# Inverse norms spread over the heads by bf16 selection matmuls in place of fp32 transposes, in a two-layer graph attention kernel

## The chip, the cores and the metric

One core of a Trainium2 chip runs the whole program. The metric is the device time of one execution in microseconds, the median of several; lower is better. Engines are named as in the profile: PE is TensorE (PEld its weight loads), DVE VectorE, ACT ScalarE, POOL GpSimd, SP SyncE, whose queue issues all DMAs.

## What is computed

128 graphs of 128 nodes with 512 features go through two pre-normed attention layers, each with a residual. The change touches only layer 0, where each node's feature vector is mapped, cut into 8 heads of 64, and normed per head to unit length; the cosine between two nodes gates the attention.

```python
m = embs @ map_w.T + map_b
sem = m.reshape(b, s, h, dk).transpose(0, 2, 1, 3)
norm = jnp.maximum(jnp.linalg.norm(sem, axis=-1, keepdims=True), COS_EPS)
n = sem / norm
cos = jnp.einsum('bhsd,bhtd->bhst', n, n)
cos_adj = (cos > THRESHOLD).astype(embs.dtype)
p_attn = jax.nn.softmax(scores, axis=-1) * keep      # scores from q and k of m
adj = cos_adj * p_attn
out = relu(((adj @ sem_h) @ gcn_W.T) / (adj.sum(-1, keepdims=True) + 1.0))
```

Layer 1 is a masked attention with 4 heads of 64 and an output projection.

## The kernel before, in words

Every matrix product with fp32 accuracy is made of three passes over f16 pairs: a tensor is kept as an upper half (rounded to f16 by ACT) and a lower half (the rest, subtracted by POOL or DVE), and PE multiplies upper by upper, upper by lower and lower by upper.

The program is unrolled over **slots**. Slot n treats graph n in its scores, cosines, softmax and gate, and works ahead or behind for the other stages. An even and the following odd slot together are a **pair**: the features of two graphs at once are made in it, with 256 moving columns. Each engine has its own hand-written list of steps per slot (`slot(s)`), and engines meet by semaphores only; an engine that waits holds everything behind it on its list. In PSUM, four banks (`unit_ps`) are given out in turn in the order of the table `UNITS`; a unit's bank is free when the step that reads it raises `unit_out`.

The order in an odd slot, as far as it matters here:

- PE (`slot`, behind L1357): scores (L1283, s_ps) and cosines (L1283, c_ps) of the slot's graph, q01, o1e (L1357), q23, weighted sums (L1323), o1o, norms (L1333), k01, lq, spread_inv_norm for graph 0 and for graph 1 (L1342), k23, lk, output (wo, L1273). The next slot, an even one, begins again with scores and cosines, then layer 1's scores, m, weighted sums, wo, va, lv, vb.
- DVE: scores_mask, q_features, o1_rows, gate (L889), o1_rows, norm_sums (L1002), attended, k_features 0 (L920), x1_stats, k_lower 0 (L943), lqk_lower of lq (L968), directions for graph 0 and 1 (L1016: m times the spread inverse norms), k_features 1, k_lower 1, lqk_lower of lk, result.
- ACT: x_rows, the exponentials (L708), o1_upper(5) and q's upper halves, e_upper, o1_upper(4) (L789, waits until the transposing DMA has read o_hl), k's upper half 0 (L797), lq's upper half (L822), the two directions_upper (L814), k's upper half 1, lk's, h1_rows, h1_upper.
- POOL: h1_lower, squares_last, keep_and_block, x_lower (L590), o1_lower(5) (L565), q_lower 0 (L597), inverse_norms, q_lower 1, e_lower (L576), directions_lower 0 and 1 (L638), norm_l1 (ve L647, nm L648, rstd L650, shift L652), o1_lower(4). In an even slot: h1_lower, v_lower, keep_and_block, result_bases (L559), p1_lower (L571), e_lower, p1_lower, norm_l1, norm_l0 (ve0, nm0, rstd0, shift0: L660, L661, L663, L665). DVE's square_rest (L1008) runs in the even slot too.
- SP: turn_h1, load_adj, load_residual, turn_x (L486, waits for x_lower), load_x, turn_o1 (L424), turn_e twice, store.

inverse_norms on POOL takes the 16 sums of squares per node (two graphs, 8 heads) to the power -1/2 (L625) and copies them out to [128 nodes, 2, 8, 64] (`inv_rows`, L631, one copy for each graph). PE then transposes inv_rows with fp32 transposes, four for each graph, so that a bank holds, for one graph, the factor of each of 512 features (rows) for each of 128 nodes (columns). The cosines wait only for the direction halves of their own graph (`dir_lo`, one count for each graph).

## Time and profile before

| | before |
|---|---|
| time, median of 3 (range) | 2671.84 us (2670.15 to 2672.61) |
| profiled execution: its time | 2665.52 us |
| profiled execution: its span | 2663.7 us, granted clock 0.981 on average |
| PE busy | 2566.1 us, 96% |
| DVE busy | 2060.3 us, 77% |
| ACT busy | 1710.0 us, 64% |
| POOL busy | 2168.1 us, 81% |
| DMA queue of all loads and turnings | 56.4% of 16 engines |
| chain that ended last | PE 89%, POOL 3%, DVE 3% |

Busy time is the sum over an engine's instructions. The granted clock is 1.00 in every stretch of 200 us from 200 to 2400 us; what is missing lies at the two ends, where the weights are prepared and the pipeline runs out. A timeline row gives start and duration in us, engine, line, operation, output and inputs, count, and in brackets the idle time before it with what ended it. Matmuls overlap in their records: 273 ns is the length of one with 256 columns, but they start 0.109 us apart.

### The profile page before, as it was taken

What the parts mean: (1) busy time and instruction counts of PE and PEld (TensorE: products, weight loads), DVE (VectorE), ACT (ScalarE), POOL (GpSimd) and SP (SyncE); (2) the same over time, 40 slices, a digit from 0 to 9 for tenths busy, and PEclk for the clock granted to TensorE, in tenths of its full rate; (3) what the DMA queues carried; (4) which work ended last, traced back from release to release, by engine and by line L of the source; (5) the groups of instructions that cost most, each with busy time, mean ns of one, the idle gap of its engine ahead of it and who ended that gap; (6) DMA issues with size and microseconds to landing.
All of it is one profiled execution on the core that took longest, in us unless ns stands there. A gap on an engine that the chain in (4) does not pass through costs nothing.

```text
span 2663.7 us, 78789 instructions
## 1 busy us (share of the span) xinstructions
PE 2566.1 (96%) x30681; PEld 2064.2 (77%) x30681; DVE 2060.3 (77%) x3456; ACT 1710.0 (64%) x4501; POOL 2168.1 (81%) x2449
## 2 busy tenths in 40 slices
PE   5789999999999999999999999999999999999995
PEld 3577888787788878878888887887888788788773
DVE  4267878878887888888788878888888878888873
ACT  1257667666766766766676676667667666766762
POOL 0368888888888888888888888888888888888873
PEclk7899999999999999999999999999999999999997
DMA  3145666556556656655665565566556556565643
GB/s 108 37 81 106 113 118 131 109 117 119 115 112 119 126 113 110 127 109 115 123 121 113 116 126 110 114 123 119 115 116 127 108 116 121 121 112 119 119 91 75
DMA packets 829123, 299.07 MB, mean 112 GB/s; under 512 B 772560, under 2 KB 778192, under 8 KB 828752
## 3 DMA queue, kind: packets, MB, share of 16 engines
q1 hardware_dynamic: 828752, 294.04, 56.4%
q8 instruction: 244, 4.00, 0.6%
q14 instruction: 127, 1.04, 0.1%
HBM read 75.80 MB, written 33.55 MB: 41 GB/s over the span
## 4 chain that ended last, share of the span: by engine, by line
PE 89%; POOL 3%; DVE 3%; ACT 2%; DMA 2%; issue 1%; SPq 1%; DVEq 0%; ACTq 0%; POOLq 0%
PE unit_ps L1265 47%; PE unit_ps L1273 24%; PE s_ps L1283 4%; PE s_ps L1323 3%; PE c_ps L1283 3%; PE unit_ps L1342 2%; PE unit_ps L1357 2%; PE unit_ps L1283 2%; PE unit_ps L1333 1%; POOL inv_norm L625 1%; DMA o_t<-o_hl 1%; ACT e_ec L708 1%; DVE qk_hl L943 1%; POOL inv_rows L631 1%; PE unit_ps L1234 1%
## 5 line engine op out<-in xcount | busy, mean ns | idle before, releaser
L708 ACT ACTIVATE e_ec<-e_ec,neg_mx 128x128 f32<-128x128 f32 x1024 | 397.9, 391 | 4.2
L1265 PE MATMUL unit_ps<-h_t,w_m_hi 128*128 128x256 f16 x2048 | 342.2, 274 | 9.5 <-DMA h_t<-h_hl 9.5
L1265 PE MATMUL unit_ps<-h_t,w_k_hi 128*128 128x256 f16 x2048 | 344.4, 273 | 0.0
L1265 PE MATMUL unit_ps<-h_t,w_q_hi 128*128 128x256 f16 x2048 | 342.8, 273 | 0.0
L1273 PE MATMUL unit_ps<-w_v_hi,h_t 128*128 128x512 f16 x1024 | 324.9, 379 | 0.0
L576 POOL TENSOR_TENSOR e_ec<-e_ec 128x1024 f16<-128x1024 f32 x128 | 287.6, 2247 | 15.7 <-ACT e_ec L735 15.7
L1265 PE MATMUL unit_ps<-h_t,w_m_lo 128*128 128x256 f16 x1024 | 280.4, 274 | 0.0
L1265 PE MATMUL unit_ps<-h_t,w_k_lo 128*128 128x256 f16 x1024 | 280.1, 274 | 0.0
L1265 PE MATMUL unit_ps<-h_t,w_q_lo 128*128 128x256 f16 x1024 | 279.1, 273 | 0.0
L943 DVE TENSOR_TENSOR qk_hl<-qk_sb,qk_hl 128x512 f16<-128x512 f32 x128 | 164.7, 1287 | 117.7 <-ACT qk_hl L797 117.6
L1265 PEld LDWEIGHTS unit_ps<-h_t,w_m_hi 128*128 128x128 f16 x2048 | 196.1, 98 | 39.0 <-issue 9.9
L920 DVE SCALAR_TENSOR_TENSOR qk_sb<-unit_ps,unscale,bias_q 128x512 f32<-128x512 f32 x128 | 96.1, 751 | 165.1 <-PE unit_ps L1265 163.8
L1265 PEld LDWEIGHTS unit_ps<-h_t,w_k_hi 128*128 128x128 f16 x2048 | 196.3, 98 | 21.8
L1265 PEld LDWEIGHTS unit_ps<-h_t,w_q_hi 128*128 128x128 f16 x2048 | 191.0, 98 | 27.2
L552 POOL TENSOR_TENSOR h_hl<-h_sb,h_hl 128x512 f16<-128x512 f32 x128 | 148.5, 1160 | 73.4 <-ACT h_hl L770 73.4
L625 POOL TENSOR_TENSOR inv_norm<-sq_sum,minus_half 128x16 f32<-128x16 f32 x64 | 186.5, 2914 | 26.4 <-DVE sq_sum L1002 26.4
L889 DVE SCALAR_TENSOR_TENSOR e_ec<-c_ps,e_ec 128x1024 f32<-128x1024 f32 x128 | 156.2, 1220 | 51.0 <-ACT e_ec L708 51.0
L708 ACT ACTIVATION_READ_ACCUMULATOR e_ec<-e_ec,neg_mx 128x1 f32 x1024 | 194.3, 190 | 0.0
L1273 PE MATMUL unit_ps<-w_v_lo,h_t 128*128 128x512 f16 x512 | 194.0, 379 | 0.0
L1273 PE MATMUL unit_ps<-w_o_hi,o_t 128*128 128x512 f16 x512 | 176.6, 386 | 14.5 <-DMA o_t<-o_hl 12.2
L1273 PEld LDWEIGHTS unit_ps<-w_v_hi,h_t 128*128 128x128 f16 x1024 | 100.2, 98 | 113.9
L797 ACT ACTIVATE qk_hl<-qk_sb 128x512 f16<-128x512 f32 x256 | 158.4, 625 | 46.4 <-DVE qk_sb L920 42.1
(175 smaller groups left out, 7722.7 us busy)
## 6 DMA issues: line engine op xcount, KB each, us to landing
xa<-in_x_dram SPq DMA_DIRECT2D x128, 256.0 KB, 3.4
xres<-in_x_dram SPq DMA_DIRECT2D x128, 256.0 KB, 2.8
out_dram<-ybuf SPq DMA_DIRECT2D x128, 256.0 KB, 2.5
h_t<-h_hl SPq DMA_TRANSPOSE x256, 3.2
ec_t<-e_ec SPq DMA_TRANSPOSE x256, 3.2
adj_in<-in_adj_dram SPq DMA_DIRECT2D x128, 16.0 KB, 2.0
p_t<-p_hl SPq DMA_TRANSPOSE x128, 3.3
o_t<-o_hl SPq DMA_TRANSPOSE x128, 3.8
```

Of the source, the lines that this page charges most:

```text
L552: nc.gpsimd.tensor_tensor(h1_hl[:, a, 1, :], h1_sb[:, a, :], h1_hl[:, a, 0, :], ALU.subtract).then_inc(h1_lo, 1)
L576: nc.gpsimd.tensor_tensor(e_hl[:, 1], e_sb[:, :, :], e_hl[:, 0], ALU.subtract).then_inc(e_lo, 1)
L625: nc.gpsimd.tensor_tensor(inv_norm[:, :], sq_sum[:, :], minus_half[:, :], ALU.pow).then_inc(inv_norm_done, 1)
L708: ins = nc.scalar.activation(e[:, h, :], e[:, h, :], ACT.Exp, bias=neg[:, h:h + 1], scale=SCALE, accum_out=sums[:, h:h + 1])
L797: nc.scalar.activation(dst[:, 0, c, :], src[:, c, :], ACT.Copy).then_inc(done, 1)
L889: nc.vector.scalar_tensor_tensor(out=e_sb[:, :, :], in0=c_ps[:, :, :].rearrange("p a (b n) -> p (a b) n", b=4), scalar=THRESHOLD * DIR_SCA ...
L920: nc.vector.scalar_tensor_tensor(out=dst[:, c0:c0 + 2, :], in0=unit_ps[:, u.bank, :].rearrange("p (c n) -> p c n", c=2), scalar=factor, in ...
L943: nc.vector.tensor_tensor(k_hl[:, 1, c, :], k_sb[:, c, :], k_hl[:, 0, c, :], ALU.subtract).then_inc(k_lo, 1)
L1265: ins = nc.tensor.matmul(out, w[a][:, i, c * P:(c + 1) * P], h[:, :, b, i, :], start=n == 0, stop=n == len(passes) - 1)
L1273: ins = nc.tensor.matmul(ps, h[:, a, i, :], w[b][:, i, :], start=n == 0, stop=n == len(passes) - 1)
L1283: ins = nc.tensor.matmul(outs[half][c], st[r, a, c, cols], mv[r, b, c, cols], start=n == 0, stop=n == 2)
L1323: ins = nc.tensor.matmul(av(p // 4)[:, p % 4, :], ec_t[:, a, p, :], v_sb[:, b, (s.n - 1) % 4, head_at(p), 0:DK + 1], start=n == 0, stop=n ...
```

## The change

The power stays. Behind it POOL splits the 16 inverse norms of a node into three bf16 parts (copy, subtract, copy, subtract: `inv_step`), in columns 0 to 23 of `inv_parts` for each of the two graphs. PE turns them with one matmul for each graph against a bf16 identity, into the unused part of the bank that `norms` has filled (`turn_inv_norm`). DVE copies these 256 columns to bf16 in SBUF (`inv_t`) and frees the bank. PE spreads them with four matmuls: `spread[:, c, :]` has ones in the rows of the three parts of heads 2c and 2c+1, so each sums the three parts and repeats them over the head's 64 features, for both graphs at once (256 columns). The banks bc0 and bc1 now hold blocks c = 0, 2 and 1, 3 of both graphs, where each held all blocks of one graph. Directions, their upper and their lower halves follow that split, so the cosines of the even slot wait for both counts of `dir_lo`. k23 moves ahead of the spread on PE, and k's second features and upper half move ahead of the directions on DVE and ACT. POOL's set-up gets two memsets, a copy and twelve selects.

```diff
-    (... ("norm", 1), ("k01", 1), ("lq", -3), ("bc0", 1), ("bc1", 1), ("k23", 1),
+    (... ("norm", 1), ("k01", 1), ("lq", -3), ("k23", 1), ("bc0", 1), ("bc1", 1),
...
+            nc.gpsimd.memset(inv_parts[:, :, :], 0.0).then_inc(ones_in, 1)
+            nc.gpsimd.memset(spread[:, :, :], 0.0).then_inc(ones_in, 1)
+            nc.gpsimd.tensor_copy(ident16[:, :], ident[:, :]).then_inc(ones_in, 1)
+            pool.wait_ge(ones_in, 5)
+            for part in range(3):
+                for c in range(C):
+                    ins = nc.gpsimd.affine_select(
+                        out=spread[:, c, :], in_=spread[:, c, :], compare_op=ALU.not_equal, fill=1.0,
+                        base=-(H * part + 2 * c), pattern=[[-1, 2], [0, DK]], channel_multiplier=1)
...
             def inverse_norms(s):
                 if s.has(1):
-                    u = s.unit("norm")
-                    pool.wait_ge(unit_out[u.bank], u.before + 1)
+                    pool.wait_ge(norm_summed, s.at(lambda t: (t + 1) // 2 + 1))
                     nc.gpsimd.tensor_tensor(inv_norm[:, :], sq_sum[:, :], minus_half[:, :], ALU.pow).then_inc(inv_norm_done, 1)
                     if s.has(-1):
-                        pool.wait_ge(unit_full, s.unit("bc1", back=2).full)
+                        pool.wait_ge(inv_turned, s.at(lambda t: (t + 1) // 2))
...
-                    for g in range(2):
-                        nc.gpsimd.tensor_copy(inv_rows[:, g], inv_norm[:, g * H:(g + 1) * H].unsqueeze(2).broadcast_to(
-                            [P, H, DK])).then_inc(inv_rows_done, 1)
+                    nc.gpsimd.tensor_copy(parts[0], inverse).then_inc(inv_step, 1)
+                    pool.wait_ge(inv_step, before + 1)
+                    nc.gpsimd.tensor_tensor(inv_rest[:, :, :], inverse, parts[0], ALU.subtract).then_inc(inv_step, 1)
+                    pool.wait_ge(inv_step, before + 2)
+                    nc.gpsimd.tensor_copy(parts[1], inv_rest[:, :, :]).then_inc(inv_step, 1)
+                    pool.wait_ge(inv_step, before + 3)
+                    nc.gpsimd.tensor_tensor(parts[2], inv_rest[:, :, :], parts[1], ALU.subtract).then_inc(inv_step, 1)
...
ACT
+                    qk_upper(s, "k", k_sb, k_hl, 1, k_hi)
                     directions_upper(s, 0)
                     directions_upper(s, 1)
-                    qk_upper(s, "k", k_sb, k_hl, 1, k_hi)
...
DVE
+            def inverse_turned(s):
+                if s.has(1):
+                    u = s.unit("norm")
+                    dve.wait_ge(inv_turned, s.at(lambda t: (t + 1) // 2 + 1))
+                    nc.vector.tensor_copy(inv_t[:, :], unit_ps[:, u.bank, P:3 * P]).then_inc(unit_out[u.bank], 1)
...
                     lqk_lower(s, "lq", lq_hl, LQ, 0)
+                    inverse_turned(s)
+                    k_features(s, 1)
                     directions(s, 0)
                     directions(s, 1)
-                    k_features(s, 1)
                     k_lower(s, 1)
...
PE
             def cosines(s):
                 if s.has(0):
-                    pe.wait_ge(dir_lo, s.at(lambda t: t + 1))
+                    pe.wait_ge(dir_lo, s.at(lambda t: 2 * (t // 2 + 1)))
...
-            def spread_inv_norm(s, g):
-                if s.has(1):
-                    pe.wait_ge(inv_rows_done, s.at(lambda t: t + 1 + g + 1))
-                    ps = start_unit(s, f"bc{g}")
+            def turn_inv_norm(s):
+                if s.has(1):
+                    pe.wait_ge(inv_step, s.at(lambda t: 4 * ((t + 1) // 2 + 1)))
+                    ps = unit_ps[:, s.unit("norm").bank]
+                    for g in range(2):
+                        ins = nc.tensor.matmul(ps[:, (g + 1) * P:(g + 2) * P], inv_parts[:, g, :], ident16[:, :],
+                                               start=True, stop=True)
+                    ins.then_inc(inv_turned, 1)
+
+            def spread_inv_norm(s):
+                if s.has(1):
+                    ps = [start_unit(s, f"bc{a}") for a in range(2)]
                     for c in range(C):
-                        ins = nc.tensor.transpose(ps[:, c * P:(c + 1) * P],
-                                                  inv_rows[:, g, 2 * c:2 * c + 2, :].rearrange("p h d -> p (h d)"), ident[:, :])
-                    ins.then_inc(unit_full, 1)
+                        ins = nc.tensor.matmul(ps[c % 2][:, c // 2 * 2 * P:(c // 2 + 1) * 2 * P], spread[:, c, :], inv_t[:, :],
+                                               start=True, stop=True)
+                        if c >= C - 2:
+                            ins.then_inc(unit_full, 1)
...
-                    spread_inv_norm(s, 0)
-                    spread_inv_norm(s, 1)
+                    turn_inv_norm(s)
                     qk_part(s, "k", w_k, 1)
+                    spread_inv_norm(s)
```

## Rows read from the trace of the kernel before

**Rows 1.** Windows: length, busy us (instructions) by engine, clock, DMA share, GB/s.

```profile
1332.79:1371.57 38.78, 38.78 (x479) 31.51 (x478) 31.35 (x54) 26.38 (x70) 33.97 (x39) 1.00 0.61 117
981.98:1022.04 40.06, 39.00 (x477) 31.43 (x476) 32.54 (x54) 26.39 (x70) 32.78 (x37) 1.00 0.63 114
280.96:2539.00 2258.04, 2252.02 (x27609) 1826.24 (x27608) 1833.64 (x3075) 1533.98 (x4060) 1963.79 (x2206) 1.00 0.60 117
```

**Rows 2.** Chain that ended last, one pair: start, us, what, count.

```profile
1320.19 5.26 PE unit_ps L1265 x48
```

**Rows 3.** Timeline of PE around the transposes of one pair.

```profile
1364.06 1.04 PE L1342 MATMUL unit_ps<-ident,inv_rows 128*128 128x128 f32 x8
1364.93 0.38 PE L1265 MATMUL unit_ps<-h_t,w_k_hi 128*128 128x256 f16 x2
```

**Rows 4.** Waits of the execution: who for whom, us, times, longest.

```profile
PE unit_ps L1265 <- DVE lq_hl L968: 9.8, 8, 1.7
...
SPq L486 <- POOL h_hl L590: 213.3, 64, 49.1
```

**Rows 5.** Timeline of POOL in the odd slot of the pair from 1332.79.

```profile
1359.99 2.91 POOL L625 TENSOR_TENSOR inv_norm<-sq_sum,minus_half 128x16 f32<-128x16 f32 x1 [0.43 <-DVE sq_sum L1002]
1363.04 1.18 POOL L631 COPY inv_rows<-inv_norm 128x512 f32<-128x512 f32 x2
1364.18 1.16 POOL L597 TENSOR_TENSOR qk_hl<-qk_sb,qk_hl 128x512 f16<-128x512 f32 x1
1365.29 2.58 POOL L576 TENSOR_TENSOR e_ec<-e_ec 128x1024 f16<-128x1024 f32 x1
1367.88 2.27 POOL L638 TENSOR_TENSOR dir_hl<-m_sb,dir_hl 128x512 f16<-128x512 f32 x2
```

**Rows 6.** Timeline of DVE in the same odd slot.

```profile
1359.40 0.42 DVE L993 TENSOR_TENSOR o_sb<-unit_ps,inv_lsum 128x256 f32<-128x256 f32 x1
...
1365.01 0.87 DVE L943 TENSOR_TENSOR qk_hl<-qk_sb,qk_hl 128x512 f16<-128x512 f32 x1 [1.74 <-ACT qk_hl L797]
1365.81 0.74 DVE L968 SCALAR_TENSOR_TENSOR lq_hl<-unit_ps,unscale,lq_hl 128x512 f16<-128x512 f32 x1
1366.47 1.27 DVE L1016 TENSOR_TENSOR m_sb<-m_sb,unit_ps 128x512 f32<-128x512 f32 x2
```

**Rows 7.** Timelines of POOL, DVE and PE in the pair from 981.98.

```profile
1014.49 2.13 POOL L576 TENSOR_TENSOR e_ec<-e_ec 128x1024 f16<-128x1024 f32 x1
...
1014.71 2.46 DVE L943 TENSOR_TENSOR qk_hl<-qk_sb,qk_hl 128x512 f16<-128x512 f32 x1 [2.05 <-ACT qk_hl L797]
...
1017.98 0.38 PE L1265 MATMUL unit_ps<-h_t,w_lk_hi 128*128 128x256 f16 x2 [1.06 <-DVE lq_hl L968]
```

**Rows 8.** Timelines of POOL and DVE in the pair from 1332.79, even slot.

```profile
1331.47 0.51 POOL L647 TENSOR_SCALAR ve<-mv 128x1 f32<-128x1 f32 x1
...
1333.04 0.19 POOL L652 TENSOR_TENSOR shift<-nm,rstd 128x1 f32<-128x1 f32 x1
...
1341.90 1.16 POOL L571 TENSOR_TENSOR p_hl<-p_sb,p_hl 128x512 f16<-128x512 f32 x1 [0.46 <-ACT p_hl L729]
...
1349.31 0.93 POOL L665 TENSOR_TENSOR shift<-nm,rstd 128x2 f32<-128x2 f32 x1
...
1354.00 2.28 POOL L590 TENSOR_TENSOR h_hl<-xa,h_hl 128x512 f16<-128x512 f32 x2
...
1348.97 1.22 DVE L1008 TENSOR_TENSOR sq_rest<-sq_t 128x1024 f32<-128x1024 f32 x1
```

**Rows 9.** Timelines of SP's queue and of ACT around the turned o_hl.

```profile
1358.99 1.20 SPq L424 DMA_TRANSPOSE o_t<-o_hl  x1
...
310.57 0.42 ACT L789 ACTIVATE o_hl<-o_sb 128x256 f16<-128x256 f32 x1 [2.02 <-DMA o_t<-o_hl]
...
2491.62 0.42 ACT L789 ACTIVATE o_hl<-o_sb 128x256 f16<-128x256 f32 x1 [4.11 <-DMA o_t<-o_hl]
```

**Rows 10.** ACT's upper halves over the execution: busy us, mean ns, idle.

```profile
L814 ACT ACTIVATE dir_hl<-m_sb 128x512 f16<-128x512 f32 x128 | 78.7, 632 | 120.3 <-DVE m_sb L1016 120.3
```

More of the change, by code:

```diff
@@ L64 @@
     (("s1a", -4), ("s1b", -4), ("m01", 2), ("m23", 2), ("wo", -5), ("va", 2), ("lv", -4), ("vb", 3)),
-    (("q01", 1), ("o1e", -5), ("q23", 1), ("o1o", -4), ("norm", 1), ("k01", 1), ("lq", -3), ("bc0", 1), ("bc1", 1), ("k23", 1),
+    (("q01", 1), ("o1e", -5), ("q23", 1), ("o1o", -4), ("norm", 1), ("k01", 1), ("lq", -3), ("k23", 1), ("bc0", 1), ("bc1", 1),
      ("lk", -3), ("wo", -5)),
@@ L236, in build @@
         sq_parts = (sq_halves[:, :, :, 1], rest_halves[:, :, :, 1], sq_halves[:, :, :, 0])
-        inv_rows = sb("inv_rows", [P, 2, H, DK])
+        inv_rest = sb("inv_rest", [P, 2, H])
+        inv_parts = sb("inv_parts", [P, 2, P], BF16)
+        inv_t = sb("inv_t", [P, 2 * P], BF16)
+        spread = sb("spread", [P, C, P], BF16)
+        ident16 = sb("ident16", [P, P], BF16)
         lq_hl = sb("lq_hl", [P, 2, C1, 2 * P], F16)
@@ L325, in build @@
         inv_norm_done = sem("inv_norm_done")
-        inv_rows_done = sem("inv_rows_done")
+        norm_summed = sem("norm_summed")
+        inv_step = sem("inv_step")
+        inv_turned = sem("inv_turned")
         masked = sem("masked")
@@ L388, in build @@
         SMALL_LOADS = 7
-        ONES = 4
+        ONES = 10
         L_AT = 2 * C
@@ L541, in _ @@
             nc.gpsimd.memset(lv_sb[:, 1, :, :, DH:DH + 1], 0.0).then_inc(ones_in, 1)
+            nc.gpsimd.memset(inv_parts[:, :, :], 0.0).then_inc(ones_in, 1)
[7 more added lines that the diff above has]
+                        base=-(H * part + 2 * c), pattern=[[-1, 2], [0, DK]], channel_multiplier=1)
+                ins.then_inc(ones_in, 1)
+                pool.wait_ge(ones_in, 6 + part)
             pool.wait_ge(largest_done, 1)
@@ L622, in inverse_norms @@
                 if s.has(1):
-                    u = s.unit("norm")
-                    pool.wait_ge(unit_out[u.bank], u.before + 1)
+                    pool.wait_ge(norm_summed, s.at(lambda t: (t + 1) // 2 + 1))
                     nc.gpsimd.tensor_tensor(inv_norm[:, :], sq_sum[:, :], minus_half[:, :], ALU.pow).then_inc(inv_norm_done, 1)
                     if s.has(-1):
-                        pool.wait_ge(unit_full, s.unit("bc1", back=2).full)
+                        pool.wait_ge(inv_turned, s.at(lambda t: (t + 1) // 2))
+                    before = s.at(lambda t: 4 * ((t + 1) // 2))
+                    inverse = inv_norm[:, :].rearrange("p (g h) -> p g h", g=2)
+                    parts = [inv_parts[:, :, H * i:H * (i + 1)] for i in range(3)]
                     pool.wait_ge(inv_norm_done, s.at(lambda t: (t + 1) // 2 + 1))
-                    settle(pool, settled_pool, s.i)
-                    for g in range(2):
-                        nc.gpsimd.tensor_copy(inv_rows[:, g], inv_norm[:, g * H:(g + 1) * H].unsqueeze(2).broadcast_to(
-                            [P, H, DK])).then_inc(inv_rows_done, 1)
+                    nc.gpsimd.tensor_copy(parts[0], inverse).then_inc(inv_step, 1)
[5 more added lines that the diff above has]
+                    nc.gpsimd.tensor_tensor(parts[2], inv_rest[:, :, :], parts[1], ALU.subtract).then_inc(inv_step, 1)
             def directions_lower(s, g):
                 if s.has(1):
-                    cols = slice(g * P, (g + 1) * P)
                     pool.wait_ge(dir_hi, s.at(lambda t: t + 1 + g + 1))
-                    nc.gpsimd.tensor_tensor(dir_hl[:, 1, :, cols], m_sb[:, :, cols], dir_hl[:, 0, :, cols],
+                    nc.gpsimd.tensor_tensor(dir_hl[:, 1, g::2, :], m_sb[:, g::2, :], dir_hl[:, 0, g::2, :],
                                             ALU.subtract).then_inc(dir_lo, 1)
@@ L812, in directions_upper @@
                         wait(act, c_full, s.at(lambda t: t + 1))
-                    cols = slice(g * P, (g + 1) * P)
-                    nc.scalar.activation(dir_hl[:, 0, :, cols], m_sb[:, :, cols], ACT.Copy).then_inc(dir_hi, 1)
+                    nc.scalar.activation(dir_hl[:, 0, g::2, :], m_sb[:, g::2, :], ACT.Copy).then_inc(dir_hi, 1)
             def lqk_upper(s, name, dst, k):
@@ L1013, in directions @@
                     u = s.unit(f"bc{g}")
-                    cols = slice(g * P, (g + 1) * P)
                     dve.wait_ge(unit_full, u.full)
-                    nc.vector.tensor_tensor(m_sb[:, :, cols], m_sb[:, :, cols],
-                                            unit_ps[:, u.bank, :].rearrange("p (c n) -> p c n", c=C),
+                    nc.vector.tensor_tensor(m_sb[:, g::2, :], m_sb[:, g::2, :],
+                                            unit_ps[:, u.bank, :].rearrange("p (c n) -> p c n", c=2),
                                             ALU.mult).then_inc(unit_out[u.bank], 1)
```

2 lines of the change are left out of this document (1 added, 1 removed).

## The prediction

> **What bounds the kernel now.** I read the windows first. In a stretch that is one pair of graphs (an even and an odd slot, from one start of the scores in an even slot to the next) the PE column equals the length of the stretch, 38.78 of 38.78 us, at a granted clock of 1.00 [rows 1]. Pairs 2 to 59 take 2258.04 us together, 38.93 on average [rows 1]: 0.15 us above the pair that has no gap. So TensorE sets the end, every column streamed costs time, and nothing else does until PE has to wait. Then I looked for what stands closest behind PE. The list of waits has PE at w_lk behind the low half of lq (DVE, L968) 8 times, and it has SyncE's queue at the turning of h (L486) behind GpSimd's x low halves in all 64 pairs [rows 4]. The timelines of one pair (start 1332.79; from here +x is us after a pair's start) give the distances. POOL ends the power at +30.11, copies inv_rows until +31.43, takes the low half of q, then that of e (2.58 us), then the two of the directions until +37.36 [rows 5]. PE starts the eight transposes at +31.27 and k23 0.87 us later [rows 3]. POOL is the engine to watch, since it has 33.97 us of work in 38.78 [rows 1].
>
> **PE's own work.** Removed: 8 fp32 transposes, 0.87 us, 0.109 each [rows 3]. Added: 4 spread matmuls with 256 moving bf16 columns. 48 f16 matmuls of 256 columns took 5.26 us, 0.11 each [rows 2], so 0.44 us. The 2 turning matmuls have 128 columns: half of that is 0.055; the bounds are nothing and the 0.109 of a transpose [rows 3]. I take 0.055, since cost here goes by columns: 0.11 together (0 to 0.22). Sum 0.55 for 0.87: 0.32 us less a pair (0.21 to 0.43), 18.6 us over the 58 pairs, some 20 in all. Everything below is what can eat this.
>
> **The wait for the three parts.** PE now waits for four small POOL operations in a chain in place of one copy. The nearest rows are shift, 0.19 us for one element, with a gap of some 0.08 before it [rows 8], and, far above, 0.59 for a copy of 512 [rows 5]. From +30.25: four at 0.19 to 0.22 and three gaps come to 1.05, so +31.30, and PE can turn at +31.36 in place of +31.27: 0.09 us lost (0 to 0.3). Behind the turn nothing else on PE is early: a plain pair becomes 38.78 - 0.32 + 0.09 = 38.55 us.
>
> **The wait for inv_t.** The spread stands one k23 (24 matmuls, 2.62 us) behind the turn: +31.36 + 0.11 + 2.62 = +34.09. Its operand is copied by DVE behind k's first low half and lq's low half, which ended +33.76 in this pair [rows 6]. The copy of 256 PSUM elements isn't in the trace; the 256-element o_sb took 0.42, and 512 elements of lq_hl took 0.74 [rows 6]: 0.42, with 0.74 as the upper bound and 0.3, where the line through both has its lower reach at some 160 elements, as the lower. It ends at about +34.0: in a plain pair just in time. Before, the thing that waited for lq's low half was w_lk at +34.76, so 1.0 us of slack is gone and 0.3 us of copy is put in.
>
> **What a late pair costs.** k's low half (L943) took 0.87 us here and 2.46 us in the late pair [rows 6, 7]: there it was issued after POOL's e_ec had started, ran on until after e_ec had ended, and PE stood 1.06 us at w_lk [rows 7]. That pair took 40.06 us, 1.28 more than a plain one [rows 1]. The Trainium skill says why ("SBUF — State Buffer", section "Who interferes with whom"): a DVE instruction with two SBUF inputs and a GpSimd instruction that reads SBUF exclude one another, and the one that came first keeps the port to its end. The trace agrees, in both directions (shift0 took 0.93 us under DVE's sq_rest, its like 0.19 [rows 8]). After the change, in such a pair: POOL's q half ends +32.42, e_ec (2.13 [rows 7]) +34.5, k's half 0.55 later, lq's half +35.7, the copy +36.08, PE starts the spread at +36.14 in place of +34.09. A late pair loses 2.05 us and takes 40.6.
>
> **Where the moved directions put POOL.** k's second features and its upper half now come before the directions. k23's result comes at +34.30; DVE then needs 0.74 and, for the directions, 1.27 [rows 6] to +36.24, ACT's last upper half (0.63 each [rows 10]) ends +36.9, and DVE takes the port for k's second low half at about +36.2 to +36.8, ahead of POOL. POOL's two direction halves, 2.27 together [rows 5], then end at some +38.97, 0.42 after the next pair's start at +38.55, where they ended 1.42 before it. That is 1.84 us later on POOL's queue, seen from the next pair. The norm of layer 1 behind them gives 0.32 back (ve took 0.51 under the lock, else 0.19 [rows 8]), leaving 1.5. Everything on POOL's queue behind it moves. The only idle place in the even slot is 0.46 us ahead of p_hl [rows 8]; about 1.0 stays. So norm_l0 reaches its nm0 just after DVE has begun sq_rest (1348.97 [rows 8]); now only shift0 is caught by it, then three of its four steps stand behind it, and it ends some 1.15 later. With dir_lo ahead of k's half the figure at p_hl is 0.6, and the rstd0 step is still caught: 0.95 later. The queue has no idle until x's low halves (1354.00 [rows 8]). SyncE waits for these in each pair [rows 4], and turn_o1 (1358.99 [rows 9]) stands behind them, so it is issued about 1.1 us later. ACT's second o_hl, and behind it k's upper half, wait for that transfer.
>
> **How many pairs become late.** Read from ACT's timeline, o_hl L789 of o1_upper(4) starts between +29.6 (310.57) and +32.0 in 57 pairs, median +30.6; one late one is at 2491.62 [rows 9]. k's low half follows 0.97 us later and is caught by e_ec if o_hl is later than about +31.4: 7 of 57 now. Moved by 0.95 to 1.15 us it would be 60 to 75%. DMA waiting may soak up some of the move, so I take 60%: 0.4 x 38.55 + 0.6 x 40.6 = 39.78, which is 0.85 above 38.93. Times 58 = 49 us, less 1 for the pairs at the ends: +48. The new set-up on POOL (two memsets, a copy, twelve selects) runs while DVE and POOL wait for weights; I cost it at nothing (0 to 3 us if that cover is gone).
>
> The profiled execution has a span of 2663.7 and a time of 2665.52 us; the sum is a difference and I put it on the median, 2671.84: **2720 us**. With 40% late pairs it is +25, with 80% +72: 2697 to 2744.
>
> **Rivals.** (a) POOL's lateness is absorbed: if the small ends differ by half a microsecond, norm_l0 gets its steps in before sq_rest, x's low halves start on time, and late pairs stay at 7 of 57. Then 0.88 x 38.55 + 0.12 x 40.6 = 38.80, -0.13 x 58 = -8: 2664; with no late pair at all 38.55, -22: 2650. For it: each link is tenths of a microsecond, and DMA landings scatter by 2.4 us. Against it: the 1.8 us shift is three to four times the idle place. 27%. (b) The mid case, 20 to 40% late, 2673 to 2697: 10%. (c) Slower still: every pair is caught, 40.6, +97 us, 2769, if the transfer lands 2 us later; it decides where o_hl never starts before +31.4: 5%. (d) The change doesn't save on PE because a small bf16 turn costs as much as a transpose: 0.21 for 0.32 a pair, 6 us; it moves all cases and isn't one of its own. The forecast has 58%.
>
> Measurement of this kernel can tell 0.2%, 5.3 us, from no change. Faster 0.26 (most of a), same 0.08, slower 0.66. The range for 8 in 10 is 2655 to 2745; the likeliest case alone spans 2697 to 2744.
>
> **What would show it.** Right: the eight L1342 rows are gone and the turn and spread stand at 0.11 and 0.44; PE has gaps of some 2 us before the spread, put down to DVE's inv_t copy, in over a third of pairs; DVE's k low half takes over 2 us in these; POOL's norm_l0 steps are longer and x's low halves start about 1 us later after a pair's start. Wrong: pairs of 38.5 us throughout, POOL's direction halves done before the next pair's start, or turn_o1 issued at the same +26.2 as now.

## The result, and the profile after

Times are medians; each ratio is to runs of the kernel before on the same chip, with its 95% interval.

| | before | after |
|---|---|---|
| time, median (range) | 2670.99 us (2664.76 to 2674.53) | 2731.95 us (2722.3 to 2735.63) |
| ratio | | 1.0223 [1.0199, 1.0246] |
| profiled execution: span, granted clock | 2663.7 us, 0.981 | 2730.8 us, 0.980 |
| mean of pairs 2 to 59 of the profiled execution | 38.93 us | 39.89 us |
| PE busy | 2566.1 us, 96% | 2559.6 us, 94% |

The change makes the kernel 2.2% slower, 61 us. The forecast was 2720, with 2655 to 2745 around it.

First the page of after: the span, the busy time of each engine, and the shares of the chain that ended last.

```profile
span 2730.8 us, 78689 instructions
...
PE 2559.6 (94%) x30553; PEld 2033.8 (74%) x30553; DVE 2058.0 (75%) x3520; ACT 1708.8 (63%) x4501; POOL 2144.6 (79%) x2592
...
PE 44%; POOL 27%; DVE 7%; DMA 7%; issue 7%; SPq 5%; ACT 3%; ACTq 0%; POOLq 0%; DVEq 0%
```

PE is busy for 6.5 us less and the profiled execution takes 67 us more. Before, 89% of the last chain was PE; now it is 44%, and 27% is POOL. So work was taken from the engine that set the end, and the end passed to a loop through POOL. The windows of two successive pairs and of pairs 2 to 59 together (columns as in [rows 1]; pairs are numbered as in the prediction, so that pair 0 is the third of the 64 in the trace):

```profile
370.04:408.60 38.56, 38.56 (x477) 31.05 (x478) 30.75 (x55) 26.40 (x70) 33.38 (x41) 1.00 0.57 119
408.60:449.14 40.54, 38.70 (x477) 30.93 (x476) 31.26 (x55) 26.43 (x70) 33.55 (x41) 1.00 0.59 112
...
290.87:2604.27 2313.40, 2243.21 (x27493) 1797.53 (x27492) 1831.16 (x3133) 1533.20 (x4060) 1937.64 (x2321) 1.00 0.58 114
```

A plain pair has shrunk from 38.78 to 38.56 and PE still has no gap in it. A late one takes 40.54 with PE busy for 38.70. In the 58 pairs PE is idle for 70.2 of 2313.40 us (before, 6.0 of 2258.04 [rows 1]). I count a pair as late when DVE's first low half of k ends past +34.5: 38 of 58, against 5 of 58 before. The list of waits names what they wait for (who, for whom, us, times, longest):

```profile
PE unit_ps L1376 <- DVE inv_t L1029: 73.3, 40, 1.8
...
PE unit_ps L1368 <- POOL inv_parts L654: 9.3, 6, 3.7
```

L1376 is the spread, L1368 the turn. The late pair from 1443.5 shows how the wait comes about. DVE, PE and POOL, start and duration in us:

```profile
1476.11 2.46 DVE L963 TENSOR_TENSOR qk_hl<-qk_sb,qk_hl 128x512 f16<-128x512 f32 x1 [2.11 <-ACT qk_hl L818]
1478.49 0.74 DVE L988 SCALAR_TENSOR_TENSOR lq_hl<-unit_ps,unscale,lq_hl 128x512 f16<-128x512 f32 x1
1479.15 0.41 DVE L1029 CAST inv_t<-unit_ps 128x256 bf16<-128x256 f32 x1
```

```profile
1474.88 0.28 PE L1368 MATMUL unit_ps<-ident,inv_parts 128*128 128x128 bf16 x2
1475.01 0.38 PE L1291 MATMUL unit_ps<-h_t,w_k_hi 128*128 128x256 f16 x2
...
1479.62 0.61 PE L1376 MATMUL unit_ps<-inv_t,spread 128*128 128x256 bf16 x4 [1.83 <-DVE inv_t L1029]
1480.07 0.38 PE L1291 MATMUL unit_ps<-h_t,w_lk_hi 128*128 128x256 f16 x2
```

```profile
1470.72 2.92 POOL L641 TENSOR_TENSOR inv_norm<-sq_sum,minus_half 128x16 f32<-128x16 f32 x1 [0.45 <-DVE sq_sum L1022]
1473.77 0.20 POOL L648 CAST inv_parts<-inv_norm 128x16 bf16<-128x16 f32 x1
1474.05 0.22 POOL L650 TENSOR_TENSOR inv_rest<-inv_norm,inv_parts 128x16 f32<-128x16 f32 x1
...
1474.61 0.22 POOL L654 TENSOR_TENSOR inv_parts<-inv_rest,inv_parts 128x16 bf16<-128x16 f32 x1
...
1475.90 2.13 POOL L593 TENSOR_TENSOR e_ec<-e_ec 128x1024 f16<-128x1024 f32 x1
```

The three parts are done at +31.32 and the turn starts at +31.37, 0.10 later than the transposes did before. But DVE's k half was issued at 1476.11, 0.2 us after e_ec had started, and ran on until 0.54 us after its end: 2.46 us, the same length as in the one late pair read from before [rows 7]. The copy of inv_t stands two places behind it, and PE waits 1.83 us for it.

Why it is issued late is seen in the even slot. POOL in the pair from 1402.94, norm_l0:

```profile
1419.03 0.19 POOL L681 TENSOR_SCALAR ve<-mv 128x2 f32<-128x2 f32 x1
1419.30 1.13 POOL L682 TENSOR_SCALAR nm<-mv 128x2 f32<-128x2 f32 x1
1420.52 0.72 POOL L684 TENSOR_TENSOR rstd<-ve,minus_half 128x2 f32<-128x2 f32 x1
1421.32 0.19 POOL L686 TENSOR_TENSOR shift<-nm,rstd 128x2 f32<-128x2 f32 x1
```

nm, for two elements, takes 1.13 us here; it was issued at +16.4, just behind DVE's sq_rest, which starts at +16.19 in both kernels. Before, only shift0 was caught there [rows 8]. So x's low halves start at +22.33 after a plain pair instead of +21.21, the turning of o_hl is issued at a median of +27.29 instead of +26.22 [rows 9], and ACT's o_hl starts at a median of +31.70 instead of +30.57. The k half follows 0.97 us behind it and, in 38 pairs, is issued after e_ec has started.

Where the 67.0 us of span are: 58 pairs at 0.954 more make 55.3; pairs 0 and 1, both late, 3.2; the stretch before pair 0, which starts at 209.9 instead of 203.2, 6.7; the tail 1.8.

### The profile page after: what moved, and what is told of

Its sections match the earlier page's. It is cut to its first block, busy times and chain, and to the rows that moved or that the text cites. A ratio compares the mean times of both kernels' runs of the same rounds, so it can differ in the third digit from the quotient of the medians.

```text
span 2730.8 us, 78689 instructions
## 1 busy us (share of the span) xinstructions
PE 2559.6 (94%) x30553; PEld 2033.8 (74%) x30553; DVE 2058.0 (75%) x3520; ACT 1708.8 (63%) x4501; POOL 2144.6 (79%) x2592
## 3 DMA queue, kind: packets, MB, share of 16 engines
q14 instruction: 129, 1.06, 0.1%
## 4 chain that ended last, share of the span: by engine, by line
PE 44%; POOL 27%; DVE 7%; DMA 7%; issue 7%; SPq 5%; ACT 3%; ACTq 0%; POOLq 0%; DVEq 0%
PE unit_ps L1291 22%; PE unit_ps L1299 12%; DMA o_t<-o_hl 7%; DVE qk_hl L963 3%; POOL ybuf L576 3%; POOL p_hl L588 3%; POOL h_hl L607 3%; POOL h_hl L569 3%; POOL v_sb L599 2%; SPq L492 2%; POOL dir_hl L659 2%; POOL sq_t L636 2%; SPq L501 2%; PE s_ps L1309 2%; PE c_ps L1309 2%
## 5 line engine op out<-in xcount | busy, mean ns | idle before, releaser
L659 POOL TENSOR_TENSOR dir_hl<-m_sb,dir_hl 128x512 f16<-128x512 f32 x128 | 165.8, 1314 | 184.7 <-ACT dir_hl L834 184.7
L593 POOL TENSOR_TENSOR e_ec<-e_ec 128x1024 f16<-128x1024 f32 x128 | 281.7, 2201 | 10.0 <-ACT e_ec L756 10.0
L963 DVE TENSOR_TENSOR qk_hl<-qk_sb,qk_hl 128x512 f16<-128x512 f32 x128 | 149.3, 1167 | 129.1 <-ACT qk_hl L818 129.1
L810 ACT ACTIVATE o_hl<-o_sb 128x256 f16<-128x256 f32 x128 | 52.4, 409 | 257.8 <-DMA o_t<-o_hl 255.7
L783 ACT ACTIVATE h_sb<-x,shift,rstd 128x512 f32<-128x512 f32 x128 | 104.1, 813 | 170.1 <-POOL shift L673 170.1
L641 POOL TENSOR_TENSOR inv_norm<-sq_sum,minus_half 128x16 f32<-128x16 f32 x64 | 186.5, 2914 | 27.4 <-DVE sq_sum L1022 27.3
```

The lines of the kernel that those rows point to most:

```text
L593: nc.gpsimd.tensor_tensor(e_hl[:, 1], e_sb[:, :, :], e_hl[:, 0], ALU.subtract).then_inc(e_lo, 1)
L641: nc.gpsimd.tensor_tensor(inv_norm[:, :], sq_sum[:, :], minus_half[:, :], ALU.pow).then_inc(inv_norm_done, 1)
L659: nc.gpsimd.tensor_tensor(dir_hl[:, 1, g::2, :], m_sb[:, g::2, :], dir_hl[:, 0, g::2, :], ALU.subtract).then_inc(dir_lo, 1)
L783: nc.scalar.activation(h1_sb[:, a, :], x1[:, (s.n - 1) % 8, :], ACT.Relu, bias=shift1[:, 0:1], scale=rstd1[:, 0:1]).then_inc(h1_done, 1)
L963: nc.vector.tensor_tensor(k_hl[:, 1, c, :], k_sb[:, c, :], k_hl[:, 0, c, :], ALU.subtract).then_inc(k_lo, 1)
```

## The experiments

Pairs are counted as above, 58 in each kernel; the last three columns are of one profiled execution each. "Plain" and "late" are the usual (median) lengths of the two kinds. The kernel before, run beside them on the same chips, had medians from 2665.53 to 2670.99 us, so kernels are compared by their ratios where microseconds would mix chips.

| run | kernel | median us | ratio | mean pair | late | plain / late us |
|---|---|---|---|---|---|---|
| e1_copy_first | after, inv_t copied first | 2711.34 | 1.0157 [1.0137, 1.0177] | 39.51 | 42 | 38.55 / 39.87 |
| e2_norm_first | after, norm_l1 and o1_lower(4) ahead of the directions | 2696.12 | 1.0101 [1.0084, 1.0117] | 39.37 | 9 | 39.14 / 41.14 |
| e3_both | e1 and e2 | 2691.19 | 1.0076 [1.0059, 1.0092] | 39.27 | 10 | 39.14 / 40.46 |
| e8_all | e3, o1_upper(4) later, set-up later | 2683.03 | 1.0046 [1.0029, 1.0063] | 39.15 | 0 | 39.14 / none |
| e9_norm_alone | after, norm_l1 alone ahead | 2666.35 | 0.9997 [0.9984, 1.0009] | 38.86 | 7 | 38.56 / 40.57 |
| e10_all_norm_alone | e8, o1_lower(4) back behind | 2648.17 | 0.994 [0.9927, 0.9952] | 38.56 | 0 | 38.56 / none |
| e12_after_o1_late | after, o1_upper(4) later | 2672.67 | 1.0022 [1.0012, 1.0031] | 38.95 | 0 | 38.94 / none |
| e11_before_o1_late | before, o1_upper(4) later | 2675.33 | 1.003 [1.0017, 1.0043] | 39.08 | 0 | 39.06 / none |
| e4_order | before, only the changed order | 2683.2 | 1.0062 [1.0041, 1.0083] | 39.27 | 23 | 38.78 / 40.00 |
| e5_fill1 | before, one copy more on POOL | 2672.88 | 1.0025 [1.0006, 1.0044] | 39.28 | 22 | 38.78 / 40.06 |
| e6_fill2 | before, two copies more | 2724.98 | 1.0216 [1.0195, 1.0238] | 39.91 | 44 | 38.8 / 40.27 |
| e7_setup | before, only the new set-up | 2665.42 | 0.9998 [0.9985, 1.001] | 38.92 | 5 | 38.78 / 40.06 |

The theory: POOL's two direction halves end past the pair's end and put the norms behind them late (the lateness); the lateness reaches x's low halves and, by SyncE and the turned o_hl, ACT's o_hl and k's low half; e_ec catches that; and the inv_t copy makes what is lost there 2.0 us instead of 1.28. The first three runs cut that chain at two places.

### The copy of inv_t first

DVE, odd slot:

```diff
+                    inverse_turned(s)
                     k_lower(s, 0)
                     lqk_lower(s, "lq", lq_hl, LQ, 0)
-                    inverse_turned(s)
```

> The changed kernel with DVE's copy of inv_t moved ahead of k's first low half and lq's low half. Theory (late pairs come from GpSimd's late queue, their price from the copy's place behind DVE's port wait): still 60 to 70% late pairs, but each stalls PE only at w_lk, by about 1.25 us in place of 2.0, so a late pair takes 39.8 us in place of 40.57 and the kernel some 30 us less than the changed one, near 2703. Rival (the chain power, three parts, turn, copy is itself what delays PE): the copy then starts as soon as the turn is done, the gaps vanish wholly, pairs of 38.56 throughout, near 2660.

The waits of e1:

```profile
PE unit_ps L1291 <- DVE lq_hl L988: 54.3, 46, 1.7
```

The wait for inv_t is gone from the late pairs and the wait of before, for lq's low half [rows 4], is back in its place, 46 times. No fewer pairs are late (42, where after has 38), but a late one takes 39.87, 1.3 over a plain one, which is what it cost before [rows 1]. So the place of the copy makes a late pair dearer by 0.7, and is not why pairs are late.

### The norm of layer 1 ahead of the directions

POOL, odd slot:

```diff
+                    norm_l1(s)
+                    o1_lower(s, 4)
                     directions_lower(s, 0)
                     directions_lower(s, 1)
-                    norm_l1(s)
-                    o1_lower(s, 4)
```

> The changed kernel with norm_l1 and o1_lower(4) ahead of the two directions_lower on GpSimd in the odd slot, where GpSimd idles some 2.9 us. Theory (GpSimd's queue is late by 1.5 us because the directions end late; this passes through norm_l0 and x's low halves to the transfer of o_hl): x's low halves are back at +21.2 after a pair's start, turn_o1 at +26.2, late pairs fall from 39 of 58 to 6 to 9 of 58 at an unchanged 40.57, mean pair 38.8, the kernel near 2672. Rival (late pairs come from the new inv_norm chain and where DVE's k half falls beside it): the share of late pairs stays, near 2730.

> Both edits of the last two kernels. Theory: 6 to 9 late pairs of 58 at 39.8 us, the others 38.56, mean 38.7, near 2667 (of it some 8 us more than before at the two ends). Rival: as for the first kernel, no late pair at all.

The share of late pairs fell from 38 to 9 and 10 of 58, as expected. The time came out 24 us above what I expected in both. The waits of e2, and POOL about 401.72:

```profile
PE c_ps L1309 <- POOL dir_hl L659: 18.7, 42, 0.9
PE unit_ps L1376 <- DVE inv_t L1029: 18.3, 10, 1.8
```

```profile
401.72 0.63 POOL L673 TENSOR_TENSOR shift<-nm,rstd 128x1 f32<-128x1 f32 x1
402.31 0.67 POOL L582 TENSOR_TENSOR o_hl<-o_sb,o_hl 128x256 f16<-128x256 f32 x1
402.94 2.27 POOL L659 TENSOR_TENSOR dir_hl<-m_sb,dir_hl 128x512 f16<-128x512 f32 x2
```

A wait had taken the place of the one removed: the next slot's cosines need both directions, and o1_lower(4), 0.67 us, now stands ahead of them. Plain pairs are 39.14, 0.58 over 38.56. I had moved two functions where the argument needed one, and my expectations had not costed the second.

### The norm alone

```diff
+                    norm_l1(s)
                     directions_lower(s, 0)
                     directions_lower(s, 1)
-                    norm_l1(s)
                     o1_lower(s, 4)
```

> The changed kernel with norm_l1 alone ahead of the two directions_lower on GpSimd; o1_lower(4) stays behind them. In e2 most plain pairs took 39.14 us in place of 38.56: PE stood 0.58 us at the cosines for the directions' low halves, which o1_lower(4) had pushed 0.66 us back. Theory: without it that wait is gone, plain pairs are 38.56 to 38.6, and GpSimd's lateness is still gone, since layer 1's h no longer waits for it: x's low halves at +21.2, 5 to 10 late pairs of 58 at 40.57, mean 38.8 to 38.9, near 2675. Rival (o1_lower(4), late by the directions, keeps GpSimd late): x's low halves 0.8 to 1.1 us late and 23 to 38 late pairs, near 2715 to 2730.

The window of pairs 2 to 59 of e9 and its wait at the spread:

```profile
286.53:2540.69 2254.16, 2238.20 (x27493) 1799.92 (x27493) 1807.57 (x3133) 1521.97 (x4061) 1949.37 (x2321) 1.00 0.61 117
```

```profile
PE unit_ps L1376 <- DVE inv_t L1029: 12.8, 7, 1.8
```

One function moved on POOL's queue brings the ratio from 1.0223 to 0.9997, some 60 us: x's low halves start at +21.21 again in every pair, 7 pairs are late, and plain pairs are 38.56. The directions still end 0.58 us past the pair's end (+39.14), so it is what is queued behind them, not their own end, that makes pairs late. This shows the chain's first half. It is also rival (a) of the prediction, brought about: 7 late of 58 gave a mean of 38.86 (it said 38.80). But the kernel as a whole is level with before, where (a) had 8 us less: of the 4 us that the 58 pairs give back, the ends take all, since pair 0 starts at 209.6.

### ACT's o_hl behind k's upper half

The second half of the chain, from x's low halves to the k half, is cut by this, in after (e12) and in before (e11). ACT, odd slot:

```diff
-                    o1_upper(s, 4)
                     qk_upper(s, "k", k_sb, k_hl, 0, k_hi)
                     lqk_upper(s, "lq", lq_hl, LQ)
+                    o1_upper(s, 4)
```

> The changed kernel with the same edit alone. Theory: no late pair; k's first low half is issued at about +30.4, between the four small steps of inv_norm, and holds the port 0.55 us, so the turn is 0.5 us late: pairs of about 39.05, near 2680, although GpSimd's queue is as late as in the changed kernel. Rival (GpSimd's lateness costs by itself, by another way than the transfer of o_hl): pairs still near 39.9 on average, near 2730.

> The kernel before with ACT's o1_upper(4) behind the upper halves of k and lq, so that nothing of theirs waits for the transfer of o_hl. It asks whether the kernel before could have had the gain of e10 without the bf16 spread. Theory: no late pair is left, but DVE issues k's first low half at about +30.4 in each pair, takes the port between GpSimd's two copies of inv_norm, the second ends 0.45 us late and the second four transposes wait some 0.28: pairs of 39.06 throughout, 7 us more over 58 pairs, near 2673. Rival: PE never waits, 38.78 throughout, 9 us less, near 2657.

In e12 x's low halves are as late as in after, at +22.32, and no pair is late. So POOL's lateness makes pairs late only by way of the o_hl that ACT waits to write. All pairs take 38.94 instead of 38.56, though (I expected 39.05), and in e11 39.06, as expected. DVE and POOL in one pair of e12, POOL's row at the same place in a pair of e11, and the wait of e12:

```profile
474.57 0.66 DVE L963 TENSOR_TENSOR qk_hl<-qk_sb,qk_hl 128x512 f16<-128x512 f32 x1
...
474.70 0.60 POOL L650 TENSOR_TENSOR inv_rest<-inv_norm,inv_parts 128x16 f32<-128x16 f32 x1
```

```profile
546.72 1.63 POOL L631 COPY inv_rows<-inv_norm 128x512 f32<-128x512 f32 x2
```

```profile
PE unit_ps L1368 <- POOL inv_parts L654: 27.6, 64, 3.7
```

The k half, freed, comes so early that it now holds up POOL's splitting (0.60 for an operation that takes 0.22 in after), or, in before, the copies (1.63 for two that take 0.59 each [rows 5]); PE waits 27.6 us for the parts, over 64 pairs, instead of 9.3. So the kernel before could not have had a gain from this edit alone: e11 is 0.3% slower than before.

### All of it

Both ACT and DVE edits, norm_l1 with and without o1_lower(4) ahead of the directions, and the set-up behind the first all-reduce:

```diff
+            pool.wait_ge(largest_done, 1)
+            nc.gpsimd.partition_all_reduce(top[:, 0:1], largest[:, 0:1], P, RED.absmax).then_inc(top_done, 1)
             nc.gpsimd.memset(inv_parts[:, :, :], 0.0).then_inc(ones_in, 1)
...
-            pool.wait_ge(largest_done, 1)
-            nc.gpsimd.partition_all_reduce(top[:, 0:1], largest[:, 0:1], P, RED.absmax).then_inc(top_done, 1)
```

> Both edits, ACT's o1_upper(4) behind k's and lq's upper halves so that these no longer wait for the transfer of o_hl, and GpSimd's set-up of the selection matrices behind its first all-reduce, where it idles. Theory: k's first low half is always issued while q's low half holds the port, no late pair is left, all pairs 38.56, 21 us less than before over 58 pairs, the first pair 2 us earlier than in the changed kernel; near 2653. Rival (DMA landing isn't the cause of late pairs): the late pairs that e3 has remain, 5 to 10 us above that.

> The kernel of e8 (copy of inv_t first on DVE, ACT's o1_upper(4) behind the upper halves of k and lq, set-up behind the first all-reduce) with o1_lower(4) back behind the directions. Theory: no late pair, no wait at the cosines, every pair 38.56: 0.59 x 58 = 34 us less than e8, near 2650, 0.7% faster than before. Rival (the cosines' wait for both graphs stays, by GpSimd's port wait): 39.0 us pairs, near 2675.

The waits of e8:

```profile
PE c_ps L1309 <- POOL dir_hl L659: 28.6, 64, 1.3
```

Then the page of e10, its window of pairs 3 to 60, its wait for the directions, and POOL and DVE in one odd slot:

```profile
span 2645.9 us, 78689 instructions
...
PE 2552.0 (96%) x30553; PEld 2038.1 (77%) x30553; DVE 2015.3 (76%) x3520; ACT 1700.1 (64%) x4501; POOL 2159.2 (82%) x2592
```

```profile
322.32:2558.96 2236.64, 2236.42 (x27495) 1800.44 (x27494) 1788.09 (x3129) 1522.59 (x4057) 1946.89 (x2315) 1.00 0.61 118
```

```profile
PE c_ps L1309 <- POOL dir_hl L659: 2.9, 3, 1.1
```

```profile
1047.16 0.22 POOL L650 TENSOR_TENSOR inv_rest<-inv_norm,inv_parts 128x16 f32<-128x16 f32 x1
...
1047.72 0.22 POOL L654 TENSOR_TENSOR inv_parts<-inv_rest,inv_parts 128x16 bf16<-128x16 f32 x1
```

```profile
1048.32 0.42 DVE L1029 CAST inv_t<-unit_ps 128x256 bf16<-128x256 f32 x1 [1.21 <-PE unit_ps L1368]
1048.66 0.94 DVE L963 TENSOR_TENSOR qk_hl<-qk_sb,qk_hl 128x512 f16<-128x512 f32 x1
```

e8 has no late pair, but each waits for the cosines (39.14), and it ends 30 us above what I expected; that expectation was on record before e2 had shown the wait. e10 has neither wait: PE is busy for 2236.42 of 2236.64 us, each pair takes 38.56, and at 0.994 [0.9927, 0.9952] (2648 us, expected 2650) it beats both kernels. Its DVE waits for the turn, which comes after all three parts, before it takes up the k half: the splitting is back at 0.22, and the collision of e12 can't happen. A pair without gaps is thus 0.22 us shorter by the change, 13 us over 58; most of the rest of the 0.6% is that the 5 late pairs of before are gone too. The 2.2% came from late pairs, and these from what stood behind the directions on POOL's queue.

### Order, lateness and set-up, each alone

e4 is before, with only k23 and its followers moved ahead of the spread and the directions; the fp32 transposes stay:

```diff
-    (... ("lq", -3), ("bc0", 1), ("bc1", 1), ("k23", 1),
+    (... ("lq", -3), ("k23", 1), ("bc0", 1), ("bc1", 1),
...
+                    qk_upper(s, "k", k_sb, k_hl, 1, k_hi)
                     directions_upper(s, 0)
                     directions_upper(s, 1)
-                    qk_upper(s, "k", k_sb, k_hl, 1, k_hi)
...
+                    k_features(s, 1)
                     directions(s, 0)
                     directions(s, 1)
-                    k_features(s, 1)
...
+                    qk_part(s, "k", w_k, 1)
                     spread_inv_norm(s, 0)
                     spread_inv_norm(s, 1)
-                    qk_part(s, "k", w_k, 1)
```

> The kernel before with the order alone changed: k23 ahead of the transposes on PE, k's second features and upper half ahead of the directions on DVE and ACT; fp32 transposes and the copies of inv_norm stay. Theory (order makes GpSimd late): a plain pair stays 38.78, x's low halves 0.8 to 1.1 us later, about 60% late pairs, each 1.28 us as before since only w_lk waits: +35 us, near 2706. Rival (the three parts and the copy of inv_t are the cause): late pairs stay 5 of 58, near 2671.

The waits of e4:

```profile
PE unit_ps L1265 <- DVE lq_hl L968: 30.4, 27, 1.7
```

The order alone makes 23 pairs late and costs 0.6%: the sign is as expected and the size half of it. Plain pairs here are 0.22 longer, so the directions end exactly at the pair's end and the lateness is less: x's low halves start at +22.02 after a plain pair, 0.80 late where after has 1.12. Behind a late pair it is the other way round, +22.33 in e4 and +22.01 in after, and the means are the same (22.15 and 22.12). The edge lies later, too. A pair is late if the k half, 0.97 us behind o_hl's start, is issued after e_ec has started, and e_ec starts when POOL's low half of q ends: +32.55 in before and in e4, +32.43 in after. For o_hl that is +31.58 and +31.46. Counted by these edges, o_hl is too late in 5 pairs of before, 22 of e4 and 38 of after, where 5, 23 and 38 are late. Held against e4's edge, +31.58, after would still have 35, so the edge accounts for 3 of the 15 pairs between them. The rest lies in when o_hl starts, a median of +31.40 in e4 and +31.70 in after, for x's low halves that are equally late on average. The difference stands behind plain pairs (13 of 34 late in e4, 18 of 19 in after), where after's low halves are 0.31 later; behind late pairs it is 9 of 23 and 20 of 38, although e4's are the later ones. One profiled execution of each does not settle this, and why e4 has so few late pairs stays open.

e5 and e6 put lateness into before without touching the order: one or two copies of 512 elements (nothing reads the result) behind the directions.

```diff
+            def pool_filler(s):
+                if s.has(1):
+                    for g in range(1):
+                        nc.gpsimd.tensor_copy(filler[:, g], inv_norm[:, 0:H].unsqueeze(2).broadcast_to([P, H, DK]))
...
                     directions_lower(s, 1)
+                    pool_filler(s)
                     norm_l1(s)
```

> The kernel before with one more copy of 512 elements (0.6 us, into a tile that nothing reads) on GpSimd behind directions_lower. Theory (0.5 us of lateness is absorbed in the even slot): x's low halves stay at +21.2, late pairs 5 to 10 of 58, within 6 us of before. Rival (no threshold, each delay on GpSimd costs in proportion): about half of the effect of two copies.

> The same with two copies (1.2 us). Theory: lateness of about 1.3 us at the next pair, 0.75 behind the idle place, norm_l0's second step caught by DVE's sq_rest, x's low halves 0.8 to 1.0 later, some 60% late pairs at 40.06: +35 us (20 to 50), near 2706. Rival (GpSimd lateness isn't passed on to the transfer): within 6 us of before.

POOL in e5, norm_l0 in a pair behind a plain one (571.62 to 572.73) and in one behind a late one (1164.38, 1166.41), and DVE's sq_rest in the first of them:

```profile
571.62 0.23 POOL L667 TENSOR_SCALAR nm<-mv 128x2 f32<-128x2 f32 x1
571.93 0.72 POOL L669 TENSOR_TENSOR rstd<-ve,minus_half 128x2 f32<-128x2 f32 x1
572.73 0.81 POOL L671 TENSOR_TENSOR shift<-nm,rstd 128x2 f32<-128x2 f32 x1
...
1164.38 1.15 POOL L667 TENSOR_SCALAR nm<-mv 128x2 f32<-128x2 f32 x1
...
1166.41 0.19 POOL L671 TENSOR_TENSOR shift<-nm,rstd 128x2 f32<-128x2 f32 x1
...
572.28 1.22 DVE L1015 TENSOR_TENSOR sq_rest<-sq_t 128x1024 f32<-128x1024 f32 x1
```

The copy took 1.07 us instead of the 0.6 that I had put in. Even so, the lateness behind a plain pair stops just short of sq_rest: nm gets in, only shift is caught, and x's low halves start at +21.21 as before. Behind a late pair it is 0.8 more, nm is caught, and they start at +22.33. So lateness feeds itself: of 22 pairs behind a late one 16 are late, of 35 behind a plain one 6. The kernel's time scatters accordingly, from 2663.04 to 2686.89, and its profiled execution lies at the upper end, so its 39.28 us a pair is no mean of its runs. That feedback I had not expected; in the profiled execution 22 pairs are late where I had 5 to 10. With two copies, 1.7 us in all, x's low halves start at +22.33 behind most plain pairs (nm caught), and at about +22.9 behind all late ones, where norm_l1's shift is caught already and all four steps of norm_l0 come after sq_rest. 44 pairs are late: 58 us where I expected 35. Before's order with 1.7 us of POOL work added is as slow as after.

e7 is before with the two memsets, the copy and the twelve selects of the set-up alone:

```diff
+            nc.gpsimd.memset(inv_parts[:, :, :], 0.0).then_inc(ones_in, 1)
+            nc.gpsimd.memset(spread[:, :, :], 0.0).then_inc(ones_in, 1)
+            nc.gpsimd.tensor_copy(ident16[:, :], ident[:, :]).then_inc(ones_in, 1)
...
+                    ins = nc.gpsimd.affine_select(
```

> The kernel before with only the set-up of the change on GpSimd (two memsets, a cast, twelve selects; their tiles are not used). The profile of the changed kernel has its second pair of features start later, the first all-reduce 3.0 us later than before. Theory: the set-up itself costs 2 to 3 us of the time. Rival (the delay of the first all-reduce is a late load, the set-up is hidden): 0.

It costs nothing that can be measured: 0.9998 [0.9985, 1.001], and pair 0 starts at 202.3. That is the rival, not the 2 to 3 us that I expected.

## Why the prediction was right, step by step

**PE's own work and the wait for the parts: right.** 38.55 was forecast, 38.56 is there. In the trace the two terms can be told apart: the turn starts at +31.37 (forecast +31.36), 0.10 later than the transposes did, and the next matmul starts 0.12 us after the turn and 0.44 to 0.45 after the spread, 0.31 less than the 0.87 of before (forecast 0.32).

**The price of a late pair: right.** Spread at +36.11 (forecast +36.14), pair 40.57 (40.6). e1 shows its two parts: 1.3 us for the collision that was there before, 0.7 for the copy that now stands behind it.

**The lateness: right behind a plain pair.** The direction halves end at +38.99, 0.43 into the next pair (forecast 0.42), and x's low halves start 1.12 later (forecast 1.15). Not foreseen: behind a late pair, which 39 of the 58 are, it is 0.80 (+22.02 in the pair from 1443.51). A late pair is itself 2.0 us longer, so the directions, which end at +40.67, are only 0.1 past its end; nm gets in ahead of sq_rest and rstd is caught in its stead. It is like the case that the prediction put at 0.95, with rstd caught, and gave no share of the pairs:

```profile
1459.86 1.63 POOL L684 TENSOR_TENSOR rstd<-ve,minus_half 128x2 f32<-128x2 f32 x1
...
1465.53 2.27 POOL L607 TENSOR_TENSOR h_hl<-xa,h_hl 128x512 f16<-128x512 f32 x2
```

So a late pair is often followed by a plain one and a plain one nearly always by a late one: 20 late of 38 behind a late pair, 18 of 19 behind a plain one.

The rule about the shared port that I took from the Trainium skill ("SBUF — State Buffer", section "Who interferes with whom") is borne out in both directions: DVE's k half 2.46 us under e_ec, 0.66 where POOL does nothing large; POOL's nm 1.13 under sq_rest, 0.23 free of it (e5). The power is an exception, told in the last section.

**The share of late pairs: 66% for 60%, near in part by luck.** The way of counting holds: in after o_hl starts past +31.4 in 38 pairs, and 38 are late (in before 7 start past it and 5 are late, the edge there being +31.58). The timeline of before was misread at its low end: o_hl starts from +28.32, not +29.6, and in 58 pairs, not 57. The step to 60% had a wrong reason. With the forecast lateness of 1.15 the count of before gives 44 of 58, 76%, and I went down to 60% because DMA might soak up some of the move. It soaked up none: the mean start of x's low halves moved by 0.91 and that of o_hl by 0.97. What held the share down, as far as the counts show, is that the lateness is only 0.80 behind a late pair, which I had not foreseen (the same count gives 27 of 58 for 0.80). The mean length is 39.89 for 39.78, 6 us over 58 pairs.

**The ends: wrong, +11.7 for -1.** Pairs 0 and 1 are late too (3.2), and 1.8 lie in the tail. The other 6.7 lie before pair 0. The windows of 130 to 210 us, of before and then of after:

```profile
130.00:210.00 80.00, 69.95 (x835) 56.78 (x834) 52.53 (x82) 43.46 (x122) 55.81 (x63) 0.96 0.37 75
```

```profile
130.00:210.00 80.00, 68.19 (x727) 52.58 (x727) 47.88 (x79) 39.60 (x106) 51.43 (x59) 0.88 0.35 71
```

PE gets through 108 fewer matmuls in that stretch, at a granted clock of 0.88 instead of 0.96: the last stretch at the lower level, 1.2 GHz, ends at 180.0 in place of 164.1. By the granted clock the 80 us hold 6.4 us less of full speed, which is about what the stretch is longer. Ahead of that PE has two waits in the slot of the first graph, of before and then of after:

```profile
133.32 1.45 PE L1283 MATMUL s_ps<-qk_hl 64*128 64x128 f16 x24 [2.35 <-DVE qk_hl L943]
134.56 1.49 PE L1283 MATMUL c_ps<-dir_hl 64*128 64x128 f16 x24
```

```profile
134.91 0.84 PE L1309 MATMUL s_ps<-qk_hl 64*128 64x128 f16 x24 [2.17 <-DVE qk_hl L963]
137.04 1.46 PE L1309 MATMUL c_ps<-dir_hl 64*128 64x128 f16 x24 [1.28 <-POOL dir_hl L659]
```

The wait at the scores is there before as well; the one at the cosines is new. The set-up alone does not do it (e7, pair 0 at 202.3) and neither does the order alone (e4, 195.8). In the seven other kernels that hold the whole change pair 0 starts at 206.4 to 210.7, and the two pairs ahead of it take 36.9 to 37.4 us each, as they take 37.7 and 37.3 in after, against 35.1 and 34.8 in before. Whether the new wait brings about the longer time at 1.2 GHz or the reverse was not tried.

**Rivals.** (a), the lateness absorbed, was the right one to fear, with the right price for the pairs (38.86 for 38.80) and the ends left out: e9 has it. (c), every pair caught, did not come. (d) is excluded by the 0.12 us of the two turns and the 0.31 saved. A rival I had not named is the one that met me in e2: what is moved out of the way of the norms gets in the way of the cosines.

**The sum.** The profiled spans differ by 67.0 us where the sum had 48: 6 more from the pairs and 13 more from the ends. The medians differ by only 60 (2731.95 against the 2671.84 on which the forecast stood), since the profiled execution of before, 2665.52, lies 6 us under its median and that of after, 2732.64, on its own. The rest is the 12 us between 2720 and 2732.

## What stays open

Why o_hl can start anywhere from +28.3 to about +33: it waits for the turned transfer, which in before is issued between +25.7 and +27.4 and is done 2.6 to 5.8 us later, and no run touched the DMA queues. Since the share of late pairs is the share of that scatter beyond the edge, this is what a forecast of the share most lacks. What delays the stretch before pair 0. Why the order alone (e4) makes only 23 pairs late. How much of e10's 0.6% before could have without the bf16 spread: e11 moved only ACT's step, and no run gave DVE in before something to wait for, as the copy of inv_t does in e10. The catch of nm by sq_rest is read from traces with it (after, e5's late stretches, e6) and without it (before, e9, e10); no run moved sq_rest itself.

## What to carry to other kernels

Before moving work ahead on the engine that sets the end, write down for each other engine when its part of the moved work ends against the start of the next period, and what is queued behind it; 0.4 us past the edge made a loss of 2.2% of a change that is otherwise level with before (e9), and moving one function of four small operations was enough to get this back. When moving something out of the way, cost each instruction moved with it: 0.67 us of o1_lower(4) cost 1.0%, some 28 us (e2 against e9, by their ratios). A stall that makes its own cause worse has two regimes near its threshold, so judge it by counting late periods, not by one execution's time.
